# Den, reciprocal and evacuation one position earlier in an attention stage with a post-norm block on eight cores

## What is computed

```python
xq = (x @ wq.T).reshape(bsz, seqlen, H, HD)
xk = (x @ wk.T).reshape(bsz, seqlen, H, HD)
xv = (x @ wv.T).reshape(bsz, seqlen, H, HD)
scores = jnp.einsum('bqhd,bkhd->bhqk', xq, xk)
probs = jax.nn.softmax(scores.astype(jnp.float32), axis=-1).astype(xq.dtype)
out = jnp.einsum('bhqk,bkhd->bqhd', probs, xv).reshape(bsz, seqlen, dim)
attn = out @ wo.T
x = _layernorm(x + attn, axis=-1)
# ffn: 8 experts of rank 64, top-1 by a softmax router
h = jnp.einsum('nd,erd->ner', x_flat, A)
y = jnp.einsum('ner,eor->neo', h, B) * SCALING
sel = jnp.take_along_axis(y, expert_idx[:, None, None], axis=1)[:, 0, :]
x = _layernorm(x + sel * expert_weight[:, None], axis=-1)
```

## Time and profile before

| | us |
|---|---|
| time of the kernel before, two runs | 4569.01 and 4261.56, median 4415.28 |
| the profiled execution | 4258.51 |
| its span on the slowest core (5) | 4257.0 |
| spans of the eight cores | 4223.8 to 4257.0 |
| PE busy | 3894.0 (91%) |
| DVE busy | 2267.5 (53%) |
| ACT busy | 1391.7 (33%) |
| POOL busy | 201.6 (5%) |

### The profile page before, as it was taken

How to read it: one execution, slowest core, us unless ns; L and a number is a source line. 1 busy time by engine, 2 the same in 40 slices (tenths; PEclk the granted TensorE clock), 3 DMA queues, 4 the chain that set the end, 5 groups by cost and what they waited for, 6 DMA issues and landing times.

```text
span 4257.0 us, 52356 instructions; the slowest of 8 cores (4223.8 to 4257.0 us)
## 1 busy us (share of the span) xinstructions
PE 3894.0 (91%) x15488; PEld 1364.8 (32%) x15488; DVE 2267.5 (53%) x4060; ACT 1391.7 (33%) x1578; POOL 201.6 (5%) x327
## 2 busy tenths in 40 slices
PE   6999999999889999999999999999999999995654
PEld 2444444444312222222222222222222222442221
DVE  0000000000078888887888878888887883236554
ACT  1111111111114444444444444444444444012111
POOL 0000000000000000000000000000000000000000
PEclk9999999999859989898998989898988986997776
DMA  9444944494110110011001001101100104232002
GB/s 143 72 65 80 163 75 80 80 150 88 60 30 1 26 26 7 20 26 25 1 26 25 11 16 26 25 1 26 26 21 6 26 3 57 40 60 40 1 40 119
DMA packets 196668, 192.35 MB, mean 45 GB/s; under 512 B 79538, under 2 KB 188210, under 8 KB 192818
## 3 DMA queue, kind: packets, MB, share of 16 engines
q0 software_dynamic: 95792, 88.20, 15.5%
q1 hardware_dynamic: 100610, 100.81, 7.6%
HBM read 218.30 MB, written 58.72 MB: 65 GB/s over the span
## 4 chain that ended last, share of the span: by engine, by line
PE 86%; DVE 4%; issue 4%; ACT 3%; DMA 2%; DVEq 0%; ACTq 0%; POOL 0%; POOLq 0%; SPq 0%
PE psB L525 11%; PE psF L347 11%; PE psA L498 7%; PE psA L491 7%; PE psC L498 7%; PE psC L491 7%; PE psB L200 5%; PE psF L200 5%; PE psD L673 5%; PE psC L200 5%; PE psC L230 4%; PE psF L230 3%; PE psB L230 3%; PE psE L845 2%; DVE pa L358 2%
## 5 line engine op out<-in xcount | busy, mean ns | idle before, releaser
L358 DVE TENSOR_REDUCE pa<-psF 128x1 f32<-128x512 f32 x2048 | 1317.1, 685 | 1509.6 <-PE psF L347 1502.5
L347 PE MATMUL psF<-AB 128*128 128x512 bf16 x2048 | 731.1, 427 | 57.7 <-DVE pa L358 34.6
L475 ACT ACTIVATE AB<-psA 128x1024 bf16<-128x1024 f32 x512 | 523.8, 1023 | 733.2 <-PE psA L498 694.6
L475 ACT ACTIVATE AB<-psC 128x1024 bf16<-128x1024 f32 x512 | 523.8, 1023 | 630.7 <-PE psC L498 585.6
L525 PE MATMUL psB<-AB 128*128 128x512 bf16 x2048 | 635.5, 414 | 0.0
L423 DVE TENSOR_TENSOR acc<-acc,AB 128x1024 bf16<-128x1024 bf16 x768 | 526.7, 686 | 61.4 <-ACT AB L475 53.6
L491 PE MATMUL psA<-X,onesmb 1*128 1x512 bf16 x1024 | 345.8, 421 | 35.4 <-ACT obuf L448 30.7
L491 PE MATMUL psC<-X,onesmb 1*128 1x512 bf16 x1024 | 344.6, 419 | 32.5 <-ACT obuf L448 27.9
L347 PEld LDWEIGHTS psF<-AB 128*128 128x128 bf16 x2048 | 215.1, 105 | 459.3 <-issue 307.2
L498 PE MATMUL psA<-AB 128*128 128x512 bf16 x1024 | 349.2, 427 | 0.0
L498 PE MATMUL psC<-AB 128*128 128x512 bf16 x1024 | 346.9, 424 | 0.0
(11 more groups left out here) (81 smaller groups left out, 2118.9 us busy)
## 6 DMA issues: line engine op xcount, KB each, us to landing
C<-xTb POOLq DMA_DIRECT2D x20, 2048.0 KB, 24.0
kdram<-B SPq DMA_DIRECT2D x8, 2048.0 KB, 10.0
vdram<-B SPq DMA_DIRECT2D x32, 512.0 KB, 2.6
AB<-kdram SPq DMA_DIRECT2D x32, 512.0 KB, 4.3
AB<-vdram SPq DMA_DIRECT2D x32, 512.0 KB, 4.3
y<-obuf SPq DMA_DIRECT2D x16, 1024.0 KB, 3.9
AB<-wkT POOLq DMA_DIRECT2D x4, 2048.0 KB, 31.5
AB<-wvT POOLq DMA_DIRECT2D x4, 2048.0 KB, 29.5
```

The lines of the kernel that those rows point to most:

```text
L347: r.op("tensor", lambda eng, ga=ga, qh=qh, par=par, j=j, c=c: eng.matmul(psF[:, (ga % 2) * 512:(ga % 2 + 1) * 512], qbuf(par)[:, qh * 1024 ...
L358: r.op("vector", lambda eng, ga=ga, scc=scc: eng.reduce_max(pa[:, scc:scc + 1], psF[:, (ga % 2) * 512:(ga % 2 + 1) * 512], axis=AX.X), [(S ...
L475: r.op("scalar", lambda eng, gk=gk, slot=slot: eng.activation(ring(gk), slot[:, :], AF.Exp), [(S_["exp"], 1)])
```

## The change

Inside the attention stage, at the start of every head but the first, steps that close the head before are given other positions. Den goes from position 4 to 3 (in the list of turns and in the loop), the reciprocal from 5 to 4, the two evacuations from 6 and 7 to 5 and 6. The cascade steps 32, 33, 34, 35 ran at positions 0, 1, 2, 3; now 32 and 33 run at position 0, 34 at 1, 35 at 2. The av_q table, the loads, the statistics DMAs and everything outside the loop stay. What follows the last head (the closing of vh 31) is as before.

```diff
-            if kt == 4 and vh >= 1:
+            if kt == 3 and vh >= 1:
                 turn_of_den[vh - 1] = len(turns)
                 turns.append(("den", vh - 1))
...
-        if kt == 4 and vh >= 1:
+        if kt == 3 and vh >= 1:
             emit_den(vh - 1)
         emit_scoresB(vh, kt)
...
-        if kt == 5 and vh >= 1:
+        if kt == 4 and vh >= 1:
             emit_recip(vh - 1)
         emit_expB(vh, kt)
 
-        if kt in (0, 1, 2, 3) and vh >= 1:
-            emit_cascade(vh - 1, 32 + kt)
+        if kt == 0 and vh >= 1:
+            emit_cascade(vh - 1, 32)
+            emit_cascade(vh - 1, 33)
+        if kt == 1 and vh >= 1:
+            emit_cascade(vh - 1, 34)
+        if kt == 2 and vh >= 1:
+            emit_cascade(vh - 1, 35)
+        if kt == 5 and vh >= 1:
+            emit_evac(vh - 1, 0)
         if kt == 6 and vh >= 1:
-            emit_evac(vh - 1, 0)
-        if kt == 7 and vh >= 1:
             emit_evac(vh - 1, 1)
```

## The result

The changed kernel is slightly slower: the ratio of its runs to those of the kernel before on the same chip is 1.0091, with a 95% interval of 1.006 to 1.0121. Its profiled execution took 4301.4 us, 42.9 us more than that of the kernel before.

What follows compares the result with a forecast made beforehand. The stage was taken as VectorE-bound at 2.4 GHz and TensorE-bound at 1.2 GHz. To 4258.5 us, 31 boundaries at about 1.6 us added 50, making 4308; less a small part for core 5, 4303 us, range 4215 to 4385.

Steps and rivals of the forecast that it cites:

- the two times shown: Whole kernel before: 4569.0 us was taken as a disturbed run, 4261.6 us as the one to compare with.
- within 2%: Whole kernel: changed time within 2% of the time before, chance 0.78; faster 0.05, slower 0.17.
- The wait moves, unshortened: Head boundaries: TensorE's wait for the Ln stays about 1.9 us at 31 boundaries, now ahead of the scores of position 4.
- The longer slow stretch: Behind the wait in long heads: five positions (4 to 8), not four, at 1.2 GHz, 2.78 us each; +1.6 us a head.
- nothing moves: Rival, AV part of heads: clock comes back earlier and makes the added slow position good; about 4259 us, chance 0.22.
- a share of long heads that shifts by more than a third: Sign against the forecast, in the stage: share of heads with mean clock below 0.90, 21 of 29 before, shifts this much.
- a usual position [...] 2.06 us, against 2.07 measured: Stage at 2.4 GHz: VectorE bounds a position with two reductions and one cascade add, 2.06 us, against 2.07 measured.
- The packed cascade adds: Positions 0 to 3: the delay of about 0.6 us is taken back at position 3; alone 0, upper bound 21 us.
- The evacuation: Two VectorE multiplies moved to positions 5 and 6: psB free one position longer than needed, gain 0.
- The discount for core 5: Head 31, slowest core 5 at 0.56 clock, others spared: a small part taken off, 4308 to 4303 us.
- faster: Rival, head boundaries: clock stays up past the wait, 23 heads save 4 us each, 92 us; about 4170 us, chance 0.10.
- The price of the Trainium skill: Slow stretches: time lost is half the throttled time; 2.78 us more a head would cost 43 us over 31 boundaries.

Runs made afterwards that it cites:

- the one with AV at 6: Changed kernel with the reciprocal at position 3, ahead of that position's exp, evacuations at 4 and 5, AV restarting at 6; 0.9421, again 0.9407.
- with the Ln first: Kernel before with the reciprocal at position 4 instead of 5, so ScalarE takes Ln and Exp ahead of the exp of position 4; 0.9603.
- With the evacuation back: Changed kernel with only the two evacuations returned to positions 6 and 7; 4301.4 and 4334.6 us, no interval.
- in groups of eight: Changed kernel with reciprocal at 3, evacuations at 4 and 5, AV at 6, plus head 31's AV matmuls released at every fourth position; 0.936.

## Why the prediction was right and wrong

**Where it was wrong: the time on record.** 4303 us (4215 to 4385) was set against a measured median of 4525. The step that failed is the one on the two times shown: "The other time shown, 4569.0, [...] is of a disturbed run; 4261.6 is the one to compare with". The forecast gave executions like the first no weight, and nine of the changed kernel's 17 were of that kind, at 4525 to 4762 us. Nothing in the trace could have told how often they come. The kernel before took 4360 us and more in 3 of 16 executions on the same chip, and in 17 of 40 in the later comparisons, so it has them without the change; why they come, and whether the change makes them more frequent, stays open. Set against the other eight, whose median is 4296.6 us, the forecast of 1.01 stands beside 1.0091, and "within 2%" came true.

**That 1.01 met 1.0091 is in part luck.** From profile to profile the mean span of the eight cores grew by 44.0 us: 35.7 in the heads 1 to 29, less than the forecast's 50 at the boundaries, and 8.0 in head 31, which the forecast did not have as a cost.

**The wait moves, unshortened: right.** 1.9 us at each boundary again.

**The longer slow stretch: right in kind, and it is shown.** 13.5 us for five positions, forecast 5 x 2.78 = 13.9. Moving only AV, by one position, gives 1.4 us a head one way and 1.9 us the other, most of it by the clock, and moving AV along with the change takes the loss away.

**The size: 1.6 us a head was forecast, 1.23 measured** (75.21 less 73.98), 36 us over 29 heads. The mis-sized term is the added slow position. The positions up to the wait gave back 1.05 us, forecast 1.2; those from the wait to AV cost 2.32 us more, forecast 2.78, as not every head is slow in all five; the AV part stayed as it was on average, as forecast (-0.04 us).
Single heads leave this average both ways. In head 6 only one AV position is slow, position 10 is fast, which is the mechanism of the rival "nothing moves". The forecast let a short head fall at position 7 and last 72.6 us; head 12 falls at position 8 and stays low for three AV positions: 75.1 us. The heads of 71 us are gone, on this core and on the others (two heads of core 0 see no 1.2 GHz at all and last 69.1 us), so the prediction's own sign, a share of long heads that shifts by more than a third, did come.

**A reading that was off: "a usual position [...] 2.06 us, against 2.07 measured".** The 2.07 us is a mean over positions with two key blocks, 2.4 us, and with one, 2.0 us. The first are longer although the clock is full and VectorE has no more to do in them.

**The packed cascade adds: wrong.** "Alone: 0" measured 0.65 us a head, 1.004 as a whole, close to the upper bound of 21 us named with it. The step "the delay is taken back at position 3" failed, in two ways. Alone, a third of the delay is taken back there, 0.27 of 0.79 us, and positions 0 to 4 are 0.5 us longer; why not more is not shown. VectorE has idle time during the wait for the Ln in any case, so that adds done earlier may win nothing there, but no run tests this. In the changed kernel the statement "nothing is queued behind a new wait" was wrong as well: den comes one position after step 35, as before, but VectorE now reaches that step one position earlier with the same four adds to do, and den waits for it. Timeline, core 2, head 6:

```profile
1705.34 0.38 PE L347 MATMUL psF<-AB 128*128 128x512 bf16 x1 [0.43 <-DVE pa L358]
...
1709.06 0.59 PE L439 MATMUL psA<-acc,onesmb 128*128 128x512 bf16 x2 [0.81 <-DVE acc L423]
```

The first is passA of position 1 behind the doubled adds, the second den behind the last one. How the 36 us divide between packing (19 us when alone) and distance (40 us, 1.37 a head, when alone) stays open: the two together are less than their sum.

**The evacuation: right,** 0 within 0.12 us a head.

**The discount for core 5: wrong.** 5 us were taken off because core 5's head 31 at 0.56 was read as its own bad luck. Three cores have it in the changed kernel, and all eight with AV at 8 in the kernel before. It costs a core 18 to 29 us against the cores without it.

**The rival "faster" had the right lever in the wrong place.** A clock that stays up past the boundary is worth 92 us by its count and about as much by the runs (3.3 us a head), but it came only once the wait was gone (0.9603), not by moving it.

**The price of the Trainium skill,** half of the throttled time ("TensorE: Matmul & The Clock Gate", section Terms): 1.7 us more slow time a head in the changed kernel would make 0.85 us by it, and 1.23 were measured, the packed adds among them. From the kernel before to the one with AV at 6, 15.8 us of slow time vanish: by the rule 7.9 us, measured 8.25, of which 1.9 are the wait and some is not the clock's, so the rule is somewhat high here. Within one kernel it is cleaner: with the Ln first a mean head of 68.77 us has 4.4 us of slow time and is 1.7 us above the heads without any, and with AV at 8 it is 1.1 us for 2.8. That is 0.4 of the slow time. The trace agrees with the rule roughly, a little under its half.

## What to carry to other kernels

A short wait on TensorE can cost more than its length: here taking away 1.9 us of it kept the clock up for longer, and that gave another 3.3 us a head. Before moving the steps that close one block and open the next, look whether the order on the engine in between (here ScalarE's Ln behind an exp that is not wanted as soon) makes the wait at all, and let the dense work start right behind the closing. An earlier closing paid here only when what it frees was started earlier as well. And look at the clock by stretch: the kernels' mean clocks are close (0.889 and 0.886 on the slowest cores), those of single heads are not (0.85 to 0.95).

## What the runs showed of the hardware that was not expected

- The clock stayed at 2.4 GHz through four VectorE-bound positions without AV (8.9 us at 1.00) in the kernel with the Ln first, where it had fallen in the same positions behind a wait of 1.86 us. It fell at position 8 or 9 instead, in 213 of 232 heads.
- A stretch at 1.2 GHz can go on with TensorE busy: head 31 ran for 83 to 86 us at 0.55 to 0.56 with TensorE busy for 81.6 to 82.3 of them, on other cores from run to run, while cores with the same instructions took 49 to 67 us. With the same matmuls in groups of eight no core stayed in it (0.83 on the slowest, at most 64 us). What decides which core falls into it is not shown.
- Two profiles show a third level of the granted clock, 0.81. With the evacuation back it is on cores 2 and 3 for 161 us of the projections, and these begin head 1 some 30 us after the others. In the changed kernel with AV at 8 it is on cores 2, 3, 6 and 7 for some 1340 us ahead of the stage, and these begin head 1 some 240 us late; on the other four it comes and goes from about 2545 us on.
